# Row counts of two gather loops, copies at fixed addresses, implied waits, and paired operations in a two-layer graph kernel

## What is computed

```python
edge_index = jnp.stack([src, dst])
x = _layernorm(x + _L0_gnn_ref(x, edge_attr_2, L0_gnn_weight, L0_gnn_root_w, L0_gnn_root_b, edge_index), axis=-1)
x = _layernorm(x + _L1_gnn_ref(x, edge_weight, edge_attr_3, edge_index, L1_gnn_w1, L1_gnn_b1, L1_gnn_w2, L1_gnn_b2), axis=-1)
```

```python
messages = jnp.einsum('ek,ei,kio->eo', basis, x[row], weight)
out = jnp.zeros((x.shape[0], weight.shape[2]), dtype=x.dtype).at[col].add(messages)
```

## Time and profile before

| | us |
|---|---|
| median of 3 runs | 8986.68 (8985.92 to 8991.64) |
| the profiled execution's own time | 8985.22 |
| its span, first to last instruction | 8983.4 |
| POOL busy in the span | 6916.8 (77%) |
| PE busy | 6866.4 (76%) |
| DVE busy | 6000.8 (67%) |
| ACT busy | 2776.4 (31%) |

### The profile page before, as it was taken

How to read it: one execution, slowest core, us unless ns; L and a number is a source line. 1 busy time by engine, 2 the same in 40 slices (tenths; PEclk the granted TensorE clock), 3 DMA queues, 4 the chain that set the end, 5 groups by cost and what they waited for, 6 DMA issues and landing times. The chain is left out here.

```text
span 8983.4 us, 126395 instructions
## 1 busy us (share of the span) xinstructions
PE 6866.4 (76%) x31138; PEld 3544.0 (39%) x31138; DVE 6000.8 (67%) x15302; ACT 2776.4 (31%) x6973; POOL 6916.8 (77%) x6409
## 2 busy tenths in 40 slices
PE   6666566566556655665699999999989999999998
PEld 3333233233222322332344444444444444444444
DVE  5444444444444444444588888888888888888888
ACT  1001001010010100101355555454554555554554
POOL 7777777777777777777577777777777777777775
PEclk8667767776776777677799999999999999999999
DMA  2111111111111111111222222222222222222222
GB/s 31 15 15 15 15 15 15 15 15 15 15 15 15 15 15 15 15 15 15 51 57 59 58 57 59 58 59 58 56 59 58 57 59 58 57 60 57 58 58 52
DMA packets 697277, 337.45 MB, mean 38 GB/s; under 512 B 592399, under 2 KB 633034, under 8 KB 697004
## 3 DMA queue, kind: packets, MB, share of 16 engines
q0 software_dynamic: 266240, 210.94, 13.3%
q10 hardware_dynamic: 20480, 102.42, 4.5%
q1 hardware_dynamic: 410537, 23.86, 3.3%
HBM read 326.85 MB, written 6.40 MB: 37 GB/s over the span
## 5 line engine op out<-in xcount | busy, mean ns | idle before, releaser
L172 POOL DMA_INDIRECT rows<-table_dram,idx_a x1920 | 2121.5, 1105 | 642.4 <-issue 615.3
L172 POOL DMA_INDIRECT rows<-in_x,idx_a x1920 | 2025.0, 1055 | 589.8 <-issue 563.2
L478 DVE TENSOR_TENSOR shared<-own_ps,rows 125x1440 f32<-125x1440 f32 x640 | 1060.0, 1656 | 1868.7 <-DMA rows<-in_x,idx_b 1179.1
L601 PE MATMUL sums_all<-shared 125*64 125x289 f32 x6400 | 1949.8, 497 | 404.7 <-issue 404.5
L910 PE MATMUL sums_ps<-prods,hot 125*64 125x272 f32 x12800 | 1620.2, 399 | 183.3 <-issue 132.6
L172 POOL DMA_INDIRECT rows<-table_dram,idx_b x1280 | 1418.8, 1108 | 390.0 <-issue 362.0
L172 POOL DMA_INDIRECT rows<-in_x,idx_b x1280 | 1350.6, 1055 | 390.2 <-issue 390.2
L688 ACT ACTIVATE flat<-sums_all 64x289 f32<-64x289 f32 x640 | 261.4, 408 | 3818.9 <-PE sums_all L601 3815.7
L900 PE MATMUL radial_x<-w2p,hidden 128*125 128x384 f32 x3840 | 1410.0, 503 | 35.0 <-ACT hidden L865 33.8
L601 PEld LDWEIGHTS sums_all<-shared 125*64 125x64 f32 x6400 | 939.2, 166 | 1233.5 <-issue 853.0
L620 PE MATMUL msg_ps<-sums,wk 96*33 96x320 f32 (+1 forms) x768 | 431.5, 732 | 1277.1 <-DVE acc L487 1277.1
(11 more groups left out here) (151 smaller groups left out, 5372.4 us busy)
## 6 DMA issues: line engine op xcount, KB each, us to landing
dist_ab<-in_edge_weight ACTq DMA_DIRECT2D x128, 468.8 KB
dist_ab<-in_edge_weight ACTq DMA_DIRECT2D x128, 312.5 KB
rows<-in_x,idx_a POOLq DMA_INDIRECT x1920, 2.4
rows<-table_dram,idx_a POOLq DMA_INDIRECT x1920, 3.0
rows<-in_x,idx_b POOLq DMA_INDIRECT x1280, 2.4
rows<-table_dram,idx_b POOLq DMA_INDIRECT x1280
vec_s<-in_edge_attr SPq DMA_DIRECT2D x129, 36.6 KB
idx_a<-in_src SPq DMA_DIRECT2D x257, 7.3 KB
```

The costliest lines, as they stand in the source:

```text
L172: pool.indirect_dma_start(out=rows[u][0:n, j, 0:width], out_offset=None, in_=table, in_offset=bass.IndirectOffsetOnAxis(ap=idx[u // 3][0:n ...
L478: dve.tensor_tensor(spread[s][:, :, 0:K].rearrange("e t (k c) -> e t k c", c=C), basis[s].unsqueeze(3).to_broadcast([EP, G, 9, C]), rows[u ...
L601: last = pe.matmul(sums_ps[s][:, 0:K + 1], hot[s][:, j, :], spread[s][:, j, :], start=(j == 0), stop=(j == G - 1))
```

## The change

- `FULL_0` becomes (0, 1, 2, 3) and `FULL_1` becomes (0, 2, 4): in each unit of stage 1 four gathers take 128 rows instead of three, and in stage 2 three instead of two.
- Stage 1, DVE: basis and one-hot are built for units 0 and 1 together, 2 and 3 together, and 4 alone (`FOLDS`). For a pair they now wait for the sum of its second unit in the batch before. The one-hot reads a small tile `rel_s` at a fixed address; a copy to `rel_t`, for stage 2, is added to `prepare`. `hot_ready` goes: the one-hot comes before `spread` on the same engine.
- Stage 1, ACT and PE: `flatten` copies both units of a pair in one instruction (128 x 289), and `fold` transposes 128 columns at once, three transposes for a pair instead of six.
- Stage 2, ACT: `rel_t` of a batch is copied once to `rel_b` at a fixed address, from which the one-hots read their bias; `rho5` is filled twice a batch (units 0 to 2 behind the hidden layer of unit 0, units 3 and 4 behind the one-hot of unit 1) instead of ten copies, and no longer at the head of each unit.
- Stage 2, DVE: three waits that others imply are left out (`dots_ready`, `summed` in `products`, `prods_ready[0]` in `reduce_along`), and `rho_ready` is waited for twice a batch.

```diff
-FULL_0, FULL_1 = (0, 2, 4), (1, 3)
+FULL_0, FULL_1 = (0, 1, 2, 3), (0, 2, 4)
...
             def build(g, i, u):
                 s = u
-                f = factors[:, u * G:(u + 1) * G, :]
-
-                dve.wait_ge(summed, last_round(g, u))
-                dve.tensor_tensor(basis[s].rearrange("e t (a b) -> e t a b", b=3),
...
-                dve.wait_ge(basis_ready, done(g, u))
+                u0, n = FOLDS[FOLD_OF[u]]
+                if u == u0:
+                    tiles = slice(u * G, (u + n) * G)
+                    f = factors[:, tiles, :]
+
+                    dve.wait_ge(summed, last_round(g, u + n - 1))
+                    dve.tensor_tensor(bases[:, tiles, :].rearrange("e t (a b) -> e t a b", b=3),
...
+                    dve.wait_ge(basis_ready, g * KF + (FOLD_OF[u] + 1))
...
             def sum_edges(g, u):
                 s = u
-                pe.wait_ge(hot_ready, done(g, u))
                 pe.wait_ge(spread_ready, done(g, u))
 
-                pe.wait_ge(flat_ready, last_round(g, u))
+                if u == FOLDS[FOLD_OF[u]][0]:
+                    pe.wait_ge(flat_ready, g * KF + (FOLD_OF[u] + 1))
...
-                for w in range(n):
-                    for c in range(3):
...
+                for c in range(3):
+                    last = pe.transpose(fold_ps[k][0:CH + 1, c, :], flat[k][:, c * CH:c * CH + CH + 1], ident[0:n * WINDOW, 0:n * WINDOW])
...
+                dve.tensor_copy(rel_t[:, tiles].rearrange("e (u j) -> e u j", j=G), rel)
...
+            def copy_rho(h, i):
+
+                u0, n = DIST[h][0], DIST[h][1] - DIST[h][0]
+                tiles = bass.ds(i * (U * G) + u0 * G, n * G)
+                act.activation(rho5[h][:, :, 0:3], rho_t[:, tiles, :], ACT.Copy)
+                act.activation(rho5[h][:, :, 3:5], rho_t[:, tiles, 0:2], ACT.Copy).then_inc(rho_ready[h], 1)
...
+                    act.activation(rel_b[:, :], rel_t[:, bass.ds(i * (U * G), U * G)], ACT.Copy).then_inc(rel_ready, 1)
...
+                        if u == 0:
+                            act.wait_ge(full_ready, g * U + 3)
+                            copy_rho(0, i)
...
                 if h == 0:
                     dve.wait_ge(inputs_ready, done(g, u))
-                    dve.wait_ge(summed, freed(g, u))
```

More of the change, by code:

```diff
@@ L214, in spline_layer @@
     FOLD_AT, COLLECT_AT = (None, 1, 2, None, 0), (0, None, 1, 2, None)
+    FLAT_AT = [u0 + n - 1 for u0, n in FOLDS]
     KF = len(FOLDS)
@@ L234, in spline_layer @@
         spread = [shared[0:EP, n * A:(n + 1) * A].rearrange("e (t k) -> e t k", k=K + 1) for n in range(DEEP)]
+        hots = shared[0:EP, DEEP * A:DEEP * (A + H)].rearrange("e (t w) -> e t w", w=WINDOW)
         hot = [shared[0:EP, DEEP * A + n * H:DEEP * A + (n + 1) * H].rearrange("e (t w) -> e t w", w=WINDOW) for n in range(DEEP)]
-        flat = ring("flat", [WINDOW, K + 1], n=DEEP)
+        flat = [sbuf(f"flat{k}", [n * WINDOW, K + 1]) for k, (_, n) in enumerate(FOLDS)]
         HALVES = [((n % 2) * WINDOW, (n % 2 + 1) * WINDOW) for n in range(DEEP)]
@@ L241, in spline_layer @@
         dst_s = sbuf("dst_s", [EP, U, G], I32)
+        rel_s = sbuf("rel_s", [EP, U, G])
         pos_s = sbuf("pos_s", [EP, U, G * 2])
@@ L429, in prepare @@
                 tiles = bass.ds(i * UG, UG)
-                rel = rel_t[:, tiles].rearrange("e (u j) -> e u j", j=G)
+                rel = rel_s[:, :, :]
                 pos = pos_s[:, :, :].rearrange("e u (j c) -> e (u j) c", c=2)
@@ L466, in build @@
                 s = u
-                f = factors[:, u * G:(u + 1) * G, :]
-                dve.wait_ge(summed, last_round(g, u))
-                dve.tensor_tensor(basis[s].rearrange("e t (a b) -> e t a b", b=3),
[L471 to L475, removed]
-                dve.wait_ge(basis_ready, done(g, u))
+                u0, n = FOLDS[FOLD_OF[u]]
[4 more added lines that the diff above has]
+                    dve.tensor_tensor(bases[:, tiles, :].rearrange("e t (a b) -> e t a b", b=3),
+                                      f[:, :, 0:3].unsqueeze(3).to_broadcast([EP, n * G, 3, 3]),
+                                      f[:, :, 3:6].unsqueeze(2).to_broadcast([EP, n * G, 3, 3]), ALU.mult).then_inc(basis_ready, 1)
+                    dve.tensor_tensor(hots[:, tiles, :], window_ps.unsqueeze(1).to_broadcast([EP, n * G, WINDOW]),
+                                      rel_s[:, :, :].rearrange("e u j -> e (u j)")[:, tiles].unsqueeze(2).to_broadcast([EP, n * G, WINDOW]), ALU.is_equal)
+                    dve.wait_ge(basis_ready, g * KF + (FOLD_OF[u] + 1))
                 dve.wait_ge(rows_landed[u], g * (16 * G) + 16 * G)
@@ L605, in fold @@
                 u0, n = FOLDS[k]
-                pe.wait_ge(flat_ready, done(g, u0 + n - 1) + CREDIT)
+                pe.wait_ge(flat_ready, g * KF + (k + 1 + KF))
                 pe.wait_ge(sums_ready, g * KF + (k + 1))
                 pe.sem_inc(folds_begun, 1)
-                for w in range(n):
-                    for c in range(3):
-                        last = pe.transpose(fold_ps[k][0:CH + 1, c, w * WINDOW:(w + 1) * WINDOW], flat[u0 + w][:, c * CH:c * CH + CH + 1],
-                                            ident[0:WINDOW, 0:WINDOW])
+                for c in range(3):
+                    last = pe.transpose(fold_ps[k][0:CH + 1, c, :], flat[k][:, c * CH:c * CH + CH + 1], ident[0:n * WINDOW, 0:n * WINDOW])
                 last.then_inc(folded, 1)
@@ L682, in _, with flatten @@
             with act.Fori(0, passes) as p:
[L684 to L688, removed]
+                def flatten(g, k):
+                    u0, n = FOLDS[k]
+                    act.wait_ge(summed, done(g, u0 + n - 1) + CREDIT)
+                    act.activation(flat[k][:, :], sums_all[0:n * WINDOW, k, 0:K + 1], ACT.Copy).then_inc(flat_ready, 1)
                 def collect(g, k):
@@ L700, in body @@
                     for u in range(U):
-                        flatten(g, u)
+                        if u in FLAT_AT:
+                            flatten(g, FLAT_AT.index(u))
                         k = COLLECT_AT[u]
@@ L763, in tensor_edges @@
         hot = ring("hot1", [EP, G, WINDOW])
-        rho5 = ring("rho5", [EP, G, 5])
+        rho5 = [sbuf(f"rho5_{h}", [EP, n * G, 5]) for h, n in enumerate((3, 2))]
         one = sbuf("one", [EP, 1])
+        rel_b = sbuf("rel_b", [EP, U * G])
         red = ring("red", [P, 2 * 16])
@@ L1021, in reduce_along @@
             def reduce_along(g, u):
-                for h in range(2):
-                    dve.wait_ge(prods_ready[h], done(g, u) + CREDIT)
+                dve.wait_ge(prods_ready[1], done(g, u) + CREDIT)
                 dve.tensor_reduce(along[:, :, :], prods[SLOT[u]][:, :, 0:MUL, 0:16], AX_X, ALU.add).then_inc(along_ready, 1)
```

37 lines of the change are left out of this document (19 added, 18 removed).

## The result

The changed kernel takes 8659.05 us (median of 4 runs, 8658.39 to 8661.10), the kernel before 8987.97 us beside it (4 runs). The ratio is 0.9634, 95% interval 0.9617 to 0.9651: 3.7% faster, 1 us from the forecast. The profiled execution took 8661.1 us, its span 8659.3. This holds for the chip of that comparison.

What follows compares the result with a forecast made beforehand. POOL's issuing of gathers was taken to bound both loops. 8985.2 us less 176 (stage 1) and 154 (stage 2), plus 3 for PE's lag, gave 8658 us; range 8625 to 8780.

Steps and rivals of the forecast that it cites:

- POOL's gathers are the bound: Both loops: POOL issues gathers without a break, so its rate, 6.80 and 7.055 us a unit, is the time.
- Stage 1, -176: Stage 1 with four full gathers: 6.525 us a unit instead of 6.80, 0.275 less x 640 units = 176 us.
- Rival 2: Full gathers in a row get dearer; at 1.60 us for the third and fourth, 9106 us in all; chance 0.04.
- Stage 2, -154: Stage 2 with three full gathers: 6.815 us a unit instead of 7.055, 0.24 less x 640 = 154 us.
- The lag, +3: Stage 2: PE's lag after a first late-rows event is no longer made up and is paid once at the end, +3 us.
- All other edits at nothing: Pairing, wider flatten and fold, copies and dropped waits lie off POOL's path or in idle time: 0 us.
- The rival within it: Stage 1: each added copy of `rel_t` holds POOL up, 128 x 0.19 = 24 us, 8682 in all; chance 0.03.
- Rival 1: Stage 2: PE keeps its waits for late rows, 4482 us there, 8776 in all; partly or wholly, chance 0.13.
- TensorE's floor of 6.79: Stage 2: PE's own pace when it has fallen behind, 6.79 us a unit, 0.27 us under POOL's 7.055 before.

Runs made afterwards that it cites:

- cut kernels: Group 3: four of five tiles' sums left out on TensorE in both loops, in four kernels; the uncut kernel before took 8985.3 us beside them.
- s_all_full: Changed kernel with all five gathers of a unit full in both loops, four of five tiles' sums cut on TensorE: 8166.5 us, 0.9089 of before.
- s_rest: Changed kernel with the old lists of full gathers, four of five tiles' sums cut on TensorE: 8982.4 us, 0.9997 of before.
- s_after: Changed kernel with its own lists, four of five tiles' sums cut on TensorE: 8675.8 us, 0.9653 of before.
- s_before: Kernel before with four of five tiles' sums cut on TensorE in both loops: 8997.7 us, 1.0013 of before.
- group 2: Changed kernel and two variants (old lists; all gathers full), every matmul in place, on a slower chip where the kernel before took 10486.6 us.
- group 1: Four variants (lists alone, rest alone, five full in stage 1, all full) on a slower chip where the kernel before took 10002.8 us.
- e1_rows_only: Kernel before with only the two lists of full gathers changed, on a slower chip: 10702.4 us, 1.0690 of before.
- e3_five_full_stage1: Changed kernel with all five gathers of a unit full in stage 1, on a slower chip: 10593.4 us, 1.0584 of before.
- e2_again: Changed kernel with the old lists of full gathers, on a slower chip: 10347.5 us, 0.9859 of before.
- after_again: The changed kernel itself, timed on a slower chip: 10930.3 us, 1.0427 of the kernel before.
- e4_again: Changed kernel with all five gathers of a unit full in both loops, on a slower chip: 11132.9 us, 1.0614 of before.

## Why the prediction was right, point by point

**POOL's gathers are the bound.** Right on the chip of the result: no wait of POOL over 0.3 us in the windows of either loop after the change, and with half of TensorE's instructions gone the time stays (1.0013 of before). By busy time TensorE would bound stage 2 (92% before, 94% after), and that view misleads: POOL is busy 78% of stage 2 both times, and its 0.30 us between gathers are part of each gather.

**Stage 1, -176.** Measured -174.9, and -176.0 between the cut kernels. The price taken for a third and fourth full gather in a row, 1.25 us, is what the rows show. Rival 2 (dearer in a row) is refuted: in `s_all_full` stage 1 is 3200 full gathers in a row at a mean of 1.25.

**Stage 2, -154.** Measured -154.6. The unit is 6.813 us where 6.815 was taken. That it fits to 1 us is in part luck: 6.815 was picked between prices that gave -144 and -163, and the pair of cut kernels, where the lists alone differ, gave -130.1.

**The lag, +3.** The tail grew by 2.6 us, as sized, though the prediction's own pieces (3.2 us of waiting and 1.4 of slow matmuls) make 4.6, and it doesn't say why it took 3. The cut kernels fit a lag of TensorE: with four fifths of the sums' matmuls gone the tail is 52.0 us in `s_rest` and 51.7 in `s_after`, and doesn't grow. The pause between the loops grew by 2.8 us, which no term had; in the cut kernels it is 61.6 us in both `s_before` and `s_rest` and 60.9 in `s_after`, so the edits aren't shown to cause it. The two make 5.4 us against 3 in the sum, and the gathers' own 329.5 against 330.

**All other edits at nothing.** `s_rest` against `s_before` is -15 us, 0.2%, with intervals of 0.1% either way; nothing of it in stage 1. In the full kernels little is left for them: the units after the change (6.529 and 6.813 us) are those that the gathers' prices alone give (6.525 and 6.815). The rival within it, the added copy holding POOL up (+24 us in stage 1), is refuted: stage 1 of `s_rest`, which has the copies, ends 1 us after that of `s_before`, which hasn't. The Trainium skill ("SBUF — State Buffer", "SBUF: two separate sides") states that a float32 copy within SBUF on VectorE keeps GpSimd from writing descriptors while it runs. That doesn't show in this kernel, with 1 us in place of 24.

**Rival 1, stage 2 can't use it.** Not so: TensorE's waits for late rows fell from 136.4 to 9.1 us, and POOL never waited. TensorE's floor of 6.79 lies 0.02 us under POOL's 6.813, so no more than that was left. `s_all_full`, with that floor removed, shows that POOL goes to 6.32. That TensorE's floor really stops a full kernel at 6.79 was not measured on this chip.

**What the prediction didn't hold.** It spoke of one chip. On three chips the kernel before takes 10003, 10487 and 10530 us; the changed kernel ran on the second, 4.3% slower than before. By the traces the gathers' prices are unchanged there, and TensorE stalls: single matmuls 1.4 us apart with nothing to wait for, or some 20 us, at most 37, of silence once a batch. Then POOL waits, and a shorter POOL unit is worth nothing. The time there also grows with the number of full gathers: in group 2 from 10348 (5 of 10 in two units, one of each loop) over 10930 (7) to 11133 (10), in group 1 from 10469 (5) over 10593 (8) to 11003 (10); but `e1_rows_only` (7, 10702) lies above `e3_five_full_stage1` (8), so the number alone doesn't order them. In group 2 the growth lies mostly in stage 2: from the first gather of that stage to the end of the span are 5434.5 us (`e2_again`), 5878.3 (`after_again`) and 6096.8 (`e4_again`), and up to that gather 4921.6, 5047.8 and 5029.1. Why TensorE stalls, why on these chips, and how full gathers take part in it stays open. It wasn't settled whether the stalls vanish with the matmuls, since the cut kernels met only the chip that has none.

## What to carry to other kernels

Read the bound from waits, not from busy shares: an engine that is busy 78% with the same small gap ahead of every instruction and no other wait is at its limit, while one at 94% may not be. Where gathers bound a loop, take the price of each kind behind each kind from the timeline and write the unit as their sum; here that sum held to 1 us in 330, with some luck in stage 2. And compare on more than one chip before a gain of a few per cent is called the kernel's: with the same code and the same gather prices the sign changed from one chip to another.

## What the runs showed of the hardware that was not expected

- Three groups met chips on which the kernel before took 10003, 10487 and 10530 us against 8985 to 8988 on the others, at a granted clock of 0.80 to 0.82 over the span against 0.85. Gathers, VectorE's operations (stage 1's spread 1647 ns against 1656) and part x's matmuls (504 ns on both) take the same time; those of part y, which stand behind the stalls, take 629 ns in place of 510 in the changed kernel. Of the 2267 us by which that kernel's span is longer, 149 are busy time of TensorE and the rest its idle time.
- A gather of 128 rows costs POOL 1.25 us from start to start in stage 1 even with 3200 in a row (`s_all_full`), one of 125 rows behind it 1.50.
- With four fifths of the sums' matmuls left out, the granted clock of stage 1 is 0.50 to 0.52 (the lower level, 1.2 GHz, nearly throughout) in place of 0.72 to 0.74, and the time doesn't change. Nor did it when the clock was high: three of the ten executions of `s_before` had 0.96 to 0.97 over the span, the other seven 0.72, and all ten took 8994 to 9006 us.
- With that cut stage 2 of the changed kernel is not faster but a little slower, 6.85 against 6.81 us a unit (on another chip of the same pace): the idx_b gathers take 1070 ns on average in place of 1057. The cause wasn't looked for.
